# Second mixture of experts: two indirect DMAs in flight on GpSimd, and another merged order of the layer-0 slot

## The reference

```python
gate_scores = jax.nn.softmax(x @ Wg, axis=-1)
topk_scores, topk_idx = jax.lax.top_k(gate_scores, K)          # K = 2, E = 8
topk_scores = topk_scores / (topk_scores.sum(-1, keepdims=True) + 1e-08)
gate = jnp.einsum('bsh,ehi->bsei', x, W11)
value = jnp.einsum('bsh,ehi->bsei', x, W12)
fused = gate * jax.nn.sigmoid(gate) * value
expert_out = jnp.einsum('bsei,eih->bseh', fused, W2)
gathered = jnp.take_along_axis(expert_out, topk_idx[..., None], axis=2)
out = jnp.sum(topk_scores[..., None] * gathered, axis=2)
```

## Time and profile before

| | us |
|---|---|
| median of 3 runs (lowest, highest) | 1487.48 (1486.67, 1488.04) |
| the profiled execution | 1486.87 |
| its span, first to last instruction | 1485.1 |
| PE busy | 1315.8 (89%) |
| DVE busy | 1088.3 (73%) |
| ACT busy | 758.6 (51%) |
| POOL busy | 343.0 (23%) |

### The profile page before, as it was taken

How to read it: one execution, slowest core, us unless ns; L and a number is a source line. 1 busy time by engine, 2 the same in 40 slices (tenths; PEclk the granted TensorE clock), 3 DMA queues, 4 the chain that set the end, 5 groups by cost and what they waited for, 6 DMA issues and landing times.

```text
span 1485.1 us, 26497 instructions
## 1 busy us (share of the span) xinstructions
PE 1315.8 (89%) x8834; PEld 996.1 (67%) x8834; DVE 1088.3 (73%) x3372; ACT 758.6 (51%) x1647; POOL 343.0 (23%) x456
## 2 busy tenths in 40 slices
PE   4489999999999999889967786999999999999556
PEld 2367777777767776656645574788888888887445
DVE  5988898989888897553268565788877788777336
ACT  4226455554646455443324453666666666666233
POOL 4501111120101101000042643322222222222720
PEclk9589999999999999999988888999999999999779
DMA  2000000000000000100003202001121112100101
GB/s 98 1 1 1 1 1 1 1 1 1 2 1 1 1 1 1 44 1 0 0 1 86 69 10 78 2 8 51 58 58 58 58 58 58 58 8 8 42 16 30
DMA packets 39555, 36.21 MB, mean 24 GB/s; under 512 B 2305, under 2 KB 38145, under 8 KB 39169
## 3 DMA queue, kind: packets, MB, share of 16 engines
q1 hardware_dynamic: 37376, 30.36, 6.8%
q0 software_dynamic: 2048, 4.20, 0.9%
HBM read 26.17 MB, written 8.39 MB: 23 GB/s over the span
## 4 chain that ended last, share of the span: by engine, by line
PE 49%; DVE 6%; another core or an unknown queue 4%; issue 2%; ACT 1%; POOL 1%; DVEq 0%; ACTq 0%; POOLq 0%
PE PS L2238 9%; PE PS L2224 8%; PE PS L2165 5%; PE PS L2216 5%; PE PS L2217 4%; PE PS L2251 4%; PE PS L2258 3%; PE PS L2295 2%; PE PS L2185 2%; PE PS L1861 2%; PE PS L2266 2%; PE PS L2305 1%; PE PS L2066 1%; PE PS L2083 1%
## 5 line engine op out<-in xcount | busy, mean ns | idle before, releaser
L1084 ACT ACTIVATE pe_<-PS 128x512 f32<-128x512 f32 (+3 forms) x384 | 175.8, 488 | 152.8 <-PE PS L2066 151.4
L2224 PE MATMUL PS<-ident,PN 128*128 128x128 f32 x1152 | 182.4, 281 | 63.5 <-DVE X L1826 27.3
L1774 DVE CUSTOM_DVE_ANT_0 PS<-PS,mask_row 128x128 f32<-128x128 f32 (+7 forms) x256 | 194.0, 764 | 57.1 <-PE PS L2217 44.5
L1152 ACT ACTIVATE PN<-PS,NM 128x128 f32<-128x128 f32 (+7 forms) x256 | 189.0, 739 | 74.0 <-DVE NM L1774 41.9
L2224 PEld LDWEIGHTS PS<-ident,PN 128*128 128x128 f32 x1152 | 138.7, 144 | 105.6 <-issue 84.2
L2216 PE MATMUL PS<-KA,QA 128*128 128x512 f32 (+3 forms) x384 | 159.5, 416 | 11.6 <-ACT PN L1152 5.7
L2046 PE MATMUL PS<-kta,qta 128*128 128x512 f32 (+3 forms) x384 | 147.1, 416 | 11.2 <-DVE tmqs L1474 6.9
L2066 PE MATMUL PS<-qtb,kta 128*128 128x512 f32 (+3 forms) x384 | 136.2, 385 | 1.0 <-ACT pe_ L1084 0.9
L877 POOL TENSOR_SCALAR_AFFINE_SELECT pe_<-pe_ 128x512 f32<-128x512 f32 x64 | 40.6, 634 | 407.3 <-ACT pe_ L1084 407.3
L2217 PE MATMUL PS<-KB,QA 128*128 128x512 f32 (+3 forms) x384 | 130.7, 353 | 0.0
L967 POOL CAST KA<-RAW 64x512 fp32r<-64x512 f32 x64 | 39.1, 611 | 392.3 <-DVE RAW L1796 366.1
(11 more groups left out here) (298 smaller groups left out, 2920.1 us busy)
## 6 DMA issues: line engine op xcount, KB each, us to landing
W<-w SPq DMA_DIRECT2D x40, 384.0 KB, 4.1
W<-by_expert SPq DMA_DIRECT2D x10, 256.0 KB, 4.7
expert_out<-YS SPq DMA_DIRECT2D x10, 256.0 KB, 2.3
W<-w SPq DMA_DIRECT2D x1, 2508.0 KB, 10.8
by_expert<-WOZ SPq DMA_DIRECT2D x2, 1024.0 KB, 6.8
W<-w SPq DMA_DIRECT2D x1, 1536.0 KB, 6.0
X<-x SPq DMA_DIRECT2D x2, 512.0 KB, 4.8
out<-X SPq DMA_DIRECT2D x2, 512.0 KB, 3.2
```

What stands on the lines that cost most here:

```text
L1084: act.activation(pe_[:, h, n % 2, 0:w], PS[:, 4 + h % 2, 0:w], ACT.Exp, scale=HD0 ** -0.5)\
L1152: act.activation(prob_rows(u, r), scores_of(u), ACT.Exp, bias=NM[:, u:u + 1], scale=-1.0, accum_out=SM[:, r % 2, u:u + 1]).then_inc(score_ ...
L1774: dve.tensor_tensor_reduce(scores_of(u), scores_of(u), mask_row[:, S - w:S], -HD1 ** -0.5, -MASKED, ALU.add, ALU.min, NM[:, u:u + 1]).then ...
L2224: ins = pe.transpose(PS[:, ring_bank[item, r], (j - 4 * k) * P:(j - 4 * k + 1) * P], prob_rows(u, r)[:, j * P:(j + 1) * P], ident[:, :])
```

## The change

Scatters and gathers get two semaphores each, one for each of the token's two experts. From the second token tile on, each indirect DMA waits for the landing of the one of the tile before with the same k, that is, for the one two places back. SyncE waits for both scatter semaphores, VectorE's combination for both gather semaphores at 16 (t + 1). The string of turns of `SLOT` is another one, with the same number of each letter.

```diff
--- before.py
+++ after.py
@@ -350,8 +350,8 @@
             assert not any(left.values())
             return order
 
-        SLOT = merge(("stsftssffstsffftststsfffstffsftfffffsftfstfsstsftfstfstsffsstfstfstfttsfstssftffftffffftff"
-                 "tstsssfftssssstffstfstfststfsftsfstfsfstfstfsfstfftsfsstsstfsftffttfsftssfftsssfftfsftsf"), t=train(1) + train(0), f=FIRST0, s=SECOND0)
+        SLOT = merge(("stsftssfffffsstttffstfssfstsffftffffsftftfsstssftfsstftssftfstfftsfsttfsstsfstffffftfffts"
+                 "ftftsssftfsssfstfstfstsffststfsstfstfssftsffstsfstfftsffsstssfsftfssfsstffttfstfffttfstfs"), t=train(1) + train(0), f=FIRST0, s=SECOND0)
         SLOT_HEAD = merge(("fttftffffffftfffffffftfffftffftfftffftffffffffffffftfftfftfftffftfftfftfftffttfftfftfftfff"
                  "fft"), t=train(0), f=FIRST0)
         SLOT_TAIL = merge(("ssttssstsstsssstssssstssssstsstsststsssststststssstssssstststsssstssssstssssstssststs"), t=train(1), s=SECOND0)
@@ -543,11 +543,12 @@
         gate_tanh, hid_made = sem("m1_gate_tanh"), sem("m1_hidden")
         tok_a, tok_v, out_a, out_v = (
             sem("m1_tokens_by_act"), sem("m1_tokens_by_dve"), sem("m1_out_by_act"), sem("m1_out_by_dve"))
-        slots_cleared, dispatched, y_stored, half_combined = (
-            sem("m1_slots_cleared"), sem("m1_dispatched"), sem("m1_out_stored"), sem("m1_half_combined"))
+        slots_cleared, y_stored, half_combined = (
+            sem("m1_slots_cleared"), sem("m1_out_stored"), sem("m1_half_combined"))
         combined = two("m1_combined")
         weights_in, tokens_in = two("m1_weights_in"), two("m1_tokens_in")
-        fetched = [sem(f"m1_fetched_{t}") for t in range(NT)]
+        dispatched = [sem(f"m1_dispatched_{k}") for k in range(2)]
+        fetched = [sem(f"m1_fetched_{k}") for k in range(2)]
 
         done1 = {}
 
@@ -761,7 +762,8 @@
                     sp.dma_start(WST[:, 4 * (n % 2) + j, :].rearrange("p (a n) -> p a n", a=3),
                                  experts_in[:, :, bass.ds(at, HID)]).then_inc(weights_in[n % 2], 16)
                 if n == 0:
-                    sp.wait_ge(dispatched, 16 * 2 * NT)
+                    for k in range(2):
+                        sp.wait_ge(dispatched[k], 16 * NT)
                 after(sp, ("mt", 0), r - 2)
                 sp.dma_start(XGS[:, n % 2, :, :], by_expert[4 * n * P:4 * (n + 1) * P, :].rearrange("(c p) d -> p c d", p=P))\
                     .then_inc(tokens_in[n % 2], 16)
@@ -940,10 +942,13 @@
                 pool.wait_ge(slots_cleared, 48)
                 for t in range(TB * b, TB * (b + 1)):
                     for k in range(2):
+                        if t:
+                            pool.wait_ge(dispatched[k], 16 * t)
                         pool.indirect_dma_start(
                             by_expert[:, :], bass.IndirectOffsetOnAxis(idx[:, t, k:k + 1], 0), XM[:, t, :], None,
-                            bounds_check=SLOTS - 1, oob_is_err=False).then_inc(dispatched, 16)
-                pool.wait_ge(dispatched, 32 * TB * (b + 1))
+                            bounds_check=SLOTS - 1, oob_is_err=False).then_inc(dispatched[k], 16)
+                for k in range(2):
+                    pool.wait_ge(dispatched[k], 16 * TB * (b + 1))
 
             for item, r in rounds(POOL1):
                 kind = item[0]
@@ -982,9 +987,11 @@
             pool.wait_ge(y_stored, 16 * BATCHES)
             for t in range(NT):
                 for k in range(2):
+                    if t:
+                        pool.wait_ge(fetched[k], 16 * t)
                     pool.indirect_dma_start(YG[t // TB][:, 2 * (t % TB) + k, :], None, expert_out[:, :],
                                             bass.IndirectOffsetOnAxis(idx[:, t, k:k + 1], 0),
-                                            bounds_check=SLOTS - 1, oob_is_err=False).then_inc(fetched[t], 16)
+                                            bounds_check=SLOTS - 1, oob_is_err=False).then_inc(fetched[k], 16)
 
 
 
@@ -1737,7 +1744,8 @@
                 elif kind == "cm":
                     for t in (2 * item[1], 2 * item[1] + 1):
                         after(dve, ("x", t % TB // 2 * 2), ROUNDS - 2 + t // TB)
-                        dve.wait_ge(fetched[t], 32)
+                        for k in range(2):
+                            dve.wait_ge(fetched[k], 16 * (t + 1))
                         dve.scalar_tensor_tensor(X[:, t, :], YG[t // TB][:, 2 * (t % TB), :], w_two[:, t, 0:1], X[:, t, :],
                                                  ALU.mult, ALU.add).then_inc(half_combined, 1)
                     for t in (2 * item[1], 2 * item[1] + 1):
```

## The result

The changed kernel takes 1427.14 us (median of 4 runs, 1426.45 to 1428.85) against 1487.08 us (4 runs, 1483.24 to 1488.04): ratio 0.9605, 95% interval [0.9584, 0.9626], 60 us less. The profiled execution took 1426.45 us, its span is 1424.7 us. The forecast was 1430 and faster, in the range of 1418 to 1501, which held both signs and so says little by itself. Behind the figure the terms did not hold: the scatters gave back 15.1 us less than was taken, the gathers 7.5 and the layer-0 order 10.8 us more, and the reason was wrong. The profile shows the first, the experiments the second.

A forecast was written before the change was run, and what follows sets the result against it. TensorE was taken as the bound, busy in 89% of the span, with 63.6 us lost at three indirect-DMA bursts. 1487.5 minus 57, layer-0 order 0 and longer bursts hidden, gave 1430 us; range 1418 to 1501.

The forecast's parts named there:

- the gathers: Burst of 32 gathers in layer 1: 71.49 us between rounds' first weighing products against 37.90, so 33.6 us too long.
- the layer-0 order: New order of turns in layer 0's seven steady slots: taken as 0, bounds minus 12 and plus 7 us.
- the reason: In layer 1's bursts, the backlog of indirect DMAs handed to GpSimd makes TensorE's signals late; the change removes it.
- The stall and that pacing ends it: TensorE's late signals in layer 1's three bursts cost 63.6 us; pacing gives back 57; chance of state gone 0.36.
- The first rival: Late signals in the three bursts are unrelated to backlog; bursts only last longer: 1498 us, slower, chance 0.38.
- Partial relief: Rival: gaps between the bursts' DMAs release signals more often, half of 63.6 us back: 1460 us, chance 0.16.
- does nothing: Rival: waits pass at once, bursts look as before, only layer-0 order counts: 1487 within a few us, chance 0.10.
- The argument against: Against the 57 us: signals are released only when a burst ends, when the backlog has long been at zero.
- That just collides: 0.4 us, nothing in the sum: After the first scatter burst, the paced burst and its casts end at 861.3, next round's cast due 860.9.
- Nine tenths: Share of the three bursts' 63.6 us loss taken to come back by pacing: minus 57 us.
- opening casts within 2 us of 36.66: Sign of being right: intervals between rounds' opening casts this near the burst-free 36.66 us through both scatter bursts.
- The pair step: Two indirect DMAs on GpSimd with the waits: scatters 3.0 us, gathers 3.15; 2.9 to 3.2 a sign of being right.

The follow-up runs named there:

- Experiments 4 and 7: The changed kernel with each indirect DMA waiting for the landing four (4) or three (7) places back instead of two: 1472.75 and 1478.69 us.
- experiment 3: The changed kernel with each of the two rounds' scatters placed behind GpSimd's two casts of the second key and query half: 1414.55 us.
- experiment 9: The kernel before with the new layer-0 order and a one-element memset, waited for, ahead of each second indirect DMA: 1426.57 us.
- experiment 8: The kernel before with the new layer-0 order and four 128x41 memsets ahead of each indirect DMA: 1422.89 us.
- experiment 10: The kernel before with the new layer-0 order and a one-element memset, waited for, ahead of each fourth indirect DMA: 1438.95 and 1449.14 us.
- experiment 12: The changed kernel with scatters behind the two casts and four memsets ahead of each indirect DMA instead of landing waits: 1428.56 us.
- experiments 8 to 11: One group of runs: experiment 8, experiment 9, experiment 10, and the changed kernel without waits between scatters (1439.35 us).

## Why the prediction came out right, and where it was wrong

- **The stall and that pacing ends it: right.** No remote waits, full clock in the bursts, moves spread over the burst, as foretold. The first rival, 1498 us, was right that the late signals have nothing to do with the backlog and that the bursts get longer, and wrong that the stall would stay. Partial relief and "does nothing" fall as well. The remote waits are larger than the prediction reads them: 7.4, 7.6 and 14.8 us are not the longest, one lasts 23.8.
- **The reason: wrong.** "The early ones differ only in the backlog handed to GpSimd ... The change takes just that away." Experiments 4 and 7 take the backlog away and keep the stall. The change did two things at once, emptying the queue and stretching the steps from 2.61 to 3.0 us a pair. I booked the second as a price of 3 us a burst; it was the cure. The argument against, that the backlog had long been at zero when the signals came free, was sound and should have turned me to the pace, the one other thing that differs.
- **The scatter bursts: wrong, the step "That just collides: 0.4 us, nothing in the sum".** The loss was sized well: 30.0 us, and 27.5 by rounds of 37.9 us. Nine tenths of it should have come back, 27.0; 11.9 us did. I asked when the next round's opening casts are due, not when the two casts directly behind the burst are: VectorE had come to them at 843.8 (853.24 less its wait of 9.46), GpSimd to them at 850.6. They stood behind the burst in the kernel before too (855.69), but there VectorE was itself held by a late signal until 856.74; with the stall gone they are what is late next, 9.5 and 8.4 us. The criterion "opening casts within 2 us of 36.66" failed for this reason (45.63, 44.84), and experiment 3 gives 12.6 us by this one word. Then 4 to 6 us of the two rounds are still left, from the length of the bursts, which the prediction put at 0.4 in the first.
- **The gathers: undersized.** 33.6 us against 37.7 given back. I compared 71.49 with an ordinary round of 37.90, but this one has less work: TensorE is busy 30.88 us in it, and undisturbed it lasts 33.81 us. Nine tenths of 33.6, 30.2, was 7.5 short.
- **The layer-0 order: 0 taken, 11.5 us measured in the slots** (10.8 at the end of layer 0), near the bound of 12. The bound had the wrong reason. I took TensorE's idle 1.69 us for all there is to win; idle fell by 0.25 us and "busy" by 1.39. So busy time is not all work that an order can't touch: TensorE's products of `st` and `grc`, for one, took 305 ns each in the old order and 292 in the new (20 in a slot). Why the same matmuls took less is open; that the gain stayed under 12 is luck.
- **The pair step:** scatters 3.0 taken, 3.0 measured, plus some long pauses. Gathers 3.15 taken: 55.1 us in 31 steps is 3.56 a pair, outside the 2.9 to 3.2 that the prediction named as a sign of being right, but between the bounds of 2.63 and 3.7; the burst grew by 14.3 us instead of 8. It hid: the last window is 33.73 against 33.68 us, and VectorE doesn't wait for a landing.
- **The two rules weighed.** By the Trainium skill ("DMA: Bandwidth & Descriptors", Queues, rings and completion order) each DMA engine takes turns between the queues that have work. I had concluded from it that fewer DMAs in flight buy nothing at the DMA engines. No run contradicts that: fewer ahead alone bought nothing (experiments 4 and 7), and the engines are 14 to 18% busy in the bursts of before, 12 to 14% in those of after. The gain lies elsewhere. The depth of 8 that the Trainium skill gives ("Advanced Engine Details and Errata", Engine Queue Depths) turned out to decide nothing: with one or two DMAs ahead or twelve the time was the same.

The errors cancel: minus 57 and 0 were forecast, minus 49.6 and minus 10.8 came. That the total hit 1430 within 3 us is luck.

## What to carry to other kernels

Where long runs of indirect DMAs stand in a kernel, look for waits on TensorE that end as "remote" while TensorE had finished long ago, and space the DMAs, for instance by waits for the landing two back; mean steps of 1.6 us for the scatters and 1.8 for the gathers in place of 1.3 were worth 46 to 50 us here, and 1.57 and 1.59 (experiment 9) as much. When a stall is removed, list every instruction that is queued behind its place, with the time at which its reader wants it: the first of them is the next bound, and moving the burst one word down was worth as much as the whole other order. Size a stall against the same round undisturbed, not against a neighbour, and don't take an engine's idle time for the limit of what a reordering can give.

## What the hardware showed that I had not expected

- One engine's stream delays another's signals: with indirect DMAs each 1.29 us on GpSimd, waits of ScalarE and VectorE for TensorE's signals lasted up to 29.4 us, with the DMA engines 14 to 19% busy. At mean steps of 1.50 us a few signals are still late, from 1.57 on none. What is shared is open: nothing here looks into it. That it is TensorE's signals that suffer is read from the waits, not tested.
- Whether a long backlog does harm at a slow pace is open: GpSimd's sequencer held some ten instructions ahead in experiment 8 (3.2 us from the last move to its gather), but only two of them DMAs.
- A stop costs 0.54 us of step (1.83 against 1.29 us, medians), and a memset of 0.15 us between two indirect DMAs costs nothing, as it lies in their gap.
- Kernels with remote waits scatter more: 1438.95 and 1449.14 us in experiment 10, 1424.3 to 1431.6 in experiment 12, 1481.2 to 1489.3 for the kernel before beside experiments 8 to 11, against 0.2% for the change.
